# A graph kernel on one core: table product moved up one step and behind the masks, tail written out by hand

## The reference, cut to what matters

```python
h = relu(layernorm(x))
s = adj @ h[:, 0]
x = x + relu(h @ w_self.T + s[:, None] * w_neigh.sum(1))      # first layer
g = relu(layernorm(x))
Wh = (g @ W).reshape(n, 4, 64)                                # second layer
e = leaky_relu(sl[:, :, None] + sr.T[None]); masked by adj + eye
x = x + elu(softmax(e) @ Wh)
```

## Time and profile before

| | |
|---|---|
| median of 3 runs | 1017.08 us (1015.75 to 1019.13) |
| the profiled execution | 1017.7 us, its span 1015.9 us |
| mean granted clock of TensorE | 0.857 of full speed |
| busy: PE, DVE, ACT, POOL | 703.0, 709.7, 329.3, 398.5 us |
| last half of `adj` packed | 705.9 us into the span |
| last `write_rows` begins | 731.5 us |
| second half begins | 733.6 us |

### The profile page before, as it was taken

The page is one execution under the profiler, slowest core; times in us unless marked ns, Lnnn a source line. Parts: engine busy times, 40 slices in busy tenths (PEclk is TensorE's granted clock), DMA queues, the critical chain, the costliest instruction groups (busy, mean ns, idle before and its releaser), DMA issues.

```text
span 1015.9 us, 13279 instructions
## 1 busy us (share of the span) xinstructions
PE 703.0 (69%) x3025; PEld 465.6 (46%) x3026; DVE 709.7 (70%) x2868; ACT 329.3 (32%) x1353; POOL 398.5 (39%) x459
## 2 busy tenths in 40 slices
PE   1267777877678776787777878776536766777766
PEld 1134444544345443544444445443425655566555
DVE  6657676676766767667766676677537787778776
ACT  1023334343433434334343343333503232223221
POOL 0032323223232232322323223232277777777770
PEclk9979898889988899887888787889759799879788
DMA  9999999999999999999999999993134454444441
GB/s 301 416 421 416 424 421 426 420 423 420 425 423 422 422 421 422 407 400 419 398 424 407 416 404 408 412 416 146 55 95 130 122 149 133 132 133 132 139 120 56
DMA packets 69999, 321.93 MB, mean 317 GB/s; under 512 B 14498, under 2 KB 48721, under 8 KB 53536
## 3 DMA queue, kind: packets, MB, share of 16 engines
q1 hardware_dynamic: 44160, 293.88, 71.0%
q0 software_dynamic: 15360, 17.46, 7.0%
q10 hardware_dynamic: 10400, 9.74, 2.8%
HBM read 312.57 MB, written 17.07 MB: 324 GB/s over the span
## 4 chain that ended last, share of the span: by engine, by line
DMA 56%; PE 14%; issue 11%; POOL 11%; DVE 4%; SPq 2%; ACT 0%; POOLq 0%; ACTq 0%; DVEq 0%
DMA big<-in_adj_dram 54%; POOL big L904 11%; PE p_pack L674 10%; SPq L247 2%; PE p_u L945 2%; DMA x_rows<-in_x_dram 1%; DMA big<-row_table,lists 1%; PE p_u L946 1%; PE p_row L661 1%; DVE big L1051 0%; DVE big L1072 0%; POOLq L904 0%; PE p_row L945 0%; DVE stat L321 0%; PE p_u L639 0%
## 5 line engine op out<-in xcount | busy, mean ns | idle before, releaser
L674 PE MATMUL p_pack<-big,pack_w 128*128 128x512 fp8e5 x1024 | 307.9, 452 | 159.1 <-DMA big<-in_adj_dram 144.5
L294 POOL DMA_INDIRECT h0g<-h_table,nbr x192 | 191.7, 998 | 472.3 <-ACT nbr L528 387.1
L674 PEld LDWEIGHTS p_pack<-big,pack_w 128*128 128x128 fp8e5 x1024 | 103.4, 107 | 307.3 <-issue 228.2
L904 POOL DMA_INDIRECT big<-row_table,lists x192 | 197.9, 1031 | 75.2 <-issue 57.3
L362 DVE MAX8 tops<-p_pack 128x8 f32<-128x256 f32 x128 | 48.9, 423 | 153.1 <-PE p_pack L674 153.1
L492 ACT ACTIVATE nbr<-keys 128x2 uint32<-128x2 f32 x64 | 13.0, 203 | 373.7 <-DVE keys L397 373.7
L945 PE MATMUL p_u<-big,ident 128*128 128x256 f32 x288 | 92.6, 469 | 57.1 <-DVE big L1072 57.1
L945 PEld LDWEIGHTS p_u<-big,ident 128*128 128x128 f32 x288 | 66.3, 238 | 72.1 <-DVE big L1072 60.3
L639 PE MATMUL p_u<-wselfT,hT 128*128 128x256 f32 x256 | 78.9, 439 | 0.0
L661 PE MATMUL p_row<-w_gat_and_heads,gT 128*128 128x264 f32 x256 | 69.4, 395 | 0.6 <-ACT rows L572 0.6
L1051 DVE TENSOR_TENSOR big<-big,p_pack 128x768 f32<-128x768 f32 x64 | 58.2, 950 | 1.1
(11 more groups left out here) (145 smaller groups left out, 1338.7 us busy)
## 6 DMA issues: line engine op xcount, KB each, us to landing
big<-in_adj_dram SPq DMA_DIRECT2D x128, 2048.0 KB, 18.2
row_table<-rows ACTq DMA_DIRECT2D x64, 132.0 KB, 9.5
big<-row_table SPq DMA_DIRECT2D x32, 264.0 KB, 3.0
x_rows<-in_x_dram SPq DMA_DIRECT2D x8, 1024.0 KB, 12.4
out_dram<-big SPq DMA_DIRECT2D x32, 256.0 KB, 2.8
h0g<-h_table,nbr POOLq DMA_INDIRECT x192, 6.2
big<-row_table,lists POOLq DMA_INDIRECT x192, 2.8
big<-in_L_gnn_w_self_dram ACTq DMA_DIRECT2D x1, 256.0 KB, 5.1
```

The lines of the kernel that those rows point to most:

```text
L294: nc.gpsimd.indirect_dma_start(out=h0g[r][:, j:j + 1], out_offset=None, in_=h0_dram[:, :], in_offset=bass.IndirectOffsetOnAxis(ap=nbr[r][: ...
L674: last = nc.tensor.matmul(p_pack[:], pack_w[:, block_no, :], low_bytes(n % HALVES)[:, i, :], start=(block_no == 0), stop=(block_no == BLOC ...
L904: nc.gpsimd.indirect_dma_start(out=dst, out_offset=None, in_=row_dram[:, :], in_offset=bass.IndirectOffsetOnAxis(ap=lists[r][:, a, j:j + 1 ...
```

## The change

`table_product` goes from lag 6 at the head of the step to lag 5 between `first_places` and `pack_second`; `write_rows` goes from lag 6 to 5, behind `second_norm`. GpSimd asks for the extra neighbour of tile t-1 behind the direct ones of tile t. What comes behind the last packing is written out for each engine (`last`), with `map_extras` ahead of `update`. The `first_product` of tile 63 goes into the bank `p_pack` and waits for the last search in place of the `update` before. `sum_flags` is called once.

```diff
-            def run(eng, *stages):
+            def run(eng, *stages, last=()):
...
-                for t in range(total + max(lag for _, lag in stages)):
+                for t in range(total + (0 if last else max(lag for _, lag in stages))):
                     step(t // depth, t % depth)
+                for stage, t in last:
+                    stage(t // depth, t % depth)
...
+        def first_bank(k, r):
+            return p_pack if num(k, r) == TILES - 1 else p_first
...
-            run(pool, (gather, 0))
+            run(pool, (ask_direct, 0), (ask_extra, 1))
...
-            run(dve, (name_extras, 2), (update, 4), (map_extras, 1), (norm, 4), (search, 0), (sort, 0), (mark, 0))
+            z = TILES - 1
+            run(dve, (name_extras, 2), (update, 4), (map_extras, 1), (norm, 4), (search, 0), (sort, 0), (mark, 0),
+                last=((name_extras, z - 1), (map_extras, z), (update, z - 3), (norm, z - 3), (name_extras, z),
+                      (update, z - 2), (norm, z - 2), (update, z - 1), (norm, z - 1), (update, z), (norm, z)))
...
             run(act, (list_neighbours, 1), (count_extras, 1), (keep_maps, 2), (pick_extras, 2),
-                (first_norm, 2), (copy_hT, 3), (copy_gT, 5), (deviation, 4), (write_rows, 6), (second_norm, 4))
+                (first_norm, 2), (copy_hT, 3), (copy_gT, 5), (deviation, 4), (second_norm, 4), (write_rows, 5),
+                last=((copy_hT, z - 2), (copy_gT, z - 4), (first_norm, z - 1), (list_neighbours, z), (count_extras, z),
+                      (keep_maps, z - 1), (pick_extras, z - 1), (write_rows, z - 4), (deviation, z - 3), (copy_hT, z - 1),
+                      (second_norm, z - 3), (first_norm, z), (keep_maps, z), (pick_extras, z),
+                      (deviation, z - 2), (second_norm, z - 2), (copy_gT, z - 3), (copy_hT, z), (write_rows, z - 3),
+                      (deviation, z - 1), (second_norm, z - 1), (copy_gT, z - 2), (write_rows, z - 2),
+                      (deviation, z), (second_norm, z), (copy_gT, z - 1), (write_rows, z - 1), (copy_gT, z), (write_rows, z)))
...
-                if not (isinstance(t, int) and t == 0):
+                if t == TILES - 1:
+                    pe.wait_ge(searched, TILES)
+                elif t > 0:
...
-            run(pe, (spread_extras, 2), (turn_first, 3), (sum_flags, 3), (first_product, 4), (turn_second, 5), (table_product, 6),
-                (pack_first, 0), (first_places, 1), (pack_second, 0))
+            z = TILES - 1
+            run(pe, (spread_extras, 2), (turn_first, 3), (first_product, 4), (turn_second, 5),
+                (pack_first, 0), (first_places, 1), (table_product, 5), (pack_second, 0),
+                last=((spread_extras, z - 1), (turn_first, z - 2), (first_product, z - 3), (turn_second, z - 4),
+                      (first_places, z), (table_product, z - 4), (turn_first, z - 1), (spread_extras, z),
+                      (first_product, z - 2), (turn_second, z - 3), (table_product, z - 3), (turn_first, z),
+                      (first_product, z - 1), (turn_second, z - 2), (sum_flags, z), (first_product, z), (table_product, z - 2),
+                      (turn_second, z - 1), (table_product, z - 1), (turn_second, z), (table_product, z)))
```

More of the change, by code:

```diff
@@ L284, in gpsimd_fill_lists, with ask, ask_direct @@
             pool.wait_ge(h0_out, 16)
-            def gather(k, r):
+            def ask(r, j):
+                nc.gpsimd.indirect_dma_start(
+                    out=h0g[r][:, j:j + 1], out_offset=None, in_=h0_dram[:, :],
+                    in_offset=bass.IndirectOffsetOnAxis(ap=nbr[r][:, j:j + 1], axis=0),
+                    bounds_check=N - 1, oob_is_err=False).then_inc(h0_in[r], 16)
+            def ask_direct(k, r):
                 t = num(k, r)
@@ L291, in gather, with ask_extra @@
                 wait_alone(pool, h0g_clear, t + 1)
[L293 to L297, removed]
                 wait_alone(pool, direct_ready, t + 1)
                 for j in range(DIRECT):
-                    ask(j)
-                wait_alone(pool, extra_ready, t + 1)
-                ask(DIRECT)
-            run(pool, (gather, 0))
+                    ask(r, j)
+            def ask_extra(k, r):
+                wait_alone(pool, extra_ready, num(k, r) + 1)
+                ask(r, DIRECT)
+            run(pool, (ask_direct, 0), (ask_extra, 1))
         def vector_fill_lists(dve):
@@ L448, in update @@
                 dve.wait_ge(h0_in[r], (k + 1) * 16 * OWN)
-                step(nc.vector.scalar_tensor_tensor(stot[r][:], h0g[r][:, 0:1], h0g[r][:, 1:2], p_first[:, D:D + 1],
+                step(nc.vector.scalar_tensor_tensor(stot[r][:], h0g[r][:, 0:1], h0g[r][:, 1:2], first_bank(k, r)[:, D:D + 1],
                                                     ALU.add, ALU.add), 1)
-                step(nc.vector.scalar_tensor_tensor(y[r][:], vsum[:], stot[r][:], p_first[:, 0:D], ALU.mult, ALU.add), 2)
+                step(nc.vector.scalar_tensor_tensor(y[r][:], vsum[:], stot[r][:], first_bank(k, r)[:, 0:D], ALU.mult, ALU.add), 2)
                 step(nc.vector.scalar_tensor_tensor(x_tile(k, r), y[r][:], 0.0, x_tile(k, r), ALU.max, ALU.add), 3)
@@ L634, in first_product @@
                 pe.wait_ge(hT_ready, t + 1)
-                if not (isinstance(t, int) and t == 0):
+                if t == TILES - 1:
+                    pe.wait_ge(searched, TILES)
+                elif t > 0:
                     pe.wait_ge(upd_step, (t - 1) * UPD + 2)
                 for c in range(DC):
-                    nc.tensor.matmul(p_first[:, 0:D], hT[r][:, c * P:(c + 1) * P], wselfT[:, c, :],
+                    nc.tensor.matmul(first_bank(k, r)[:, 0:D], hT[r][:, c * P:(c + 1) * P], wselfT[:, c, :],
                                      start=(c == 0), stop=(c == DC - 1))
@@ L642, in first_product @@
                 pe.wait_ge(map_copied, t + 1)
-                nc.tensor.matmul(p_first[:, D:D + 1], map_[r][:], h0g[r][:, DIRECT:OWN], start=True, stop=True
+                nc.tensor.matmul(first_bank(k, r)[:, D:D + 1], map_[r][:], h0g[r][:, DIRECT:OWN], start=True, stop=True
                                  ).then_inc(u_ready, 1)
@@ L678, in sum_flags @@
             def sum_flags(k, r):
-                if num(k, r) != TILES - 1:
-                    return
                 pe.wait_ge(flagged, TILES)
```

## The result

The changed kernel takes **1071.44 us** (median of 3 runs, 1068.44 to 1085.22), the kernel before beside it 1017.08. The ratio is 1.0518, 95% interval 1.0481 to 1.0555: **slower by 5.2%, 54 us**. The forecast was 1036.6 with a range of 1016 to 1050: the sign was right, the size was not. The profiled execution is the longest, 14 us over the median, and counts as slow, while the ratio goes by the fast ones (1068.44 to 1071.44), so its parts add up to some 14 us more than the ratio says.

The account below looks back on a forecast made before the run. Landings of `adj` loads, 10.53 us a tile, were taken to bound the stream. 731.5 + 16 (ring) + 3.5 (tail) + 284.4 = 1035.4 us span; with 1.8 around it, less 0.6 to the median, 1036.6; range 1016 to 1050.

Parts of the forecast that it names:

- the ring: Stream: waits from second packing through `sort`, `list_neighbours`, `copy_gT` and table product to the next second packing; +16 us.
- The mean of the ring: Stream: average distance between second packings, forecast 10.8 us, 0.27 over the landings' pace, +16 us over 60 tiles.
- all low time falls on the pair: Stream: upper bound with all 2.7 us low-clock time on table product and second packing; 10.9 us a tile, +22.
- three tiles in five wholly low: Stream: bound with 0.6 of tiles at 12.2 us, mean 11.2, +40 us, 1060; grouped with a 0.05 rival.
- every pass starts slow: Stream: rival with product and packing low at every step, 12.2 us a tile, +100, 1120 us; chance 0.05.
- The loads: Stream: `adj` loads asked for later once TensorE is behind, but not lost: two tiles (21 us) against 17.8.
- The split gathers: GpSimd: extra neighbour asked for behind the direct ones lands some 2 us later, due two steps on; costs nothing.
- The tail, +3.5: After the last packing: high-clock walk of the written order gave +0.5, low stretches raised it to +3.5; bounds -4, +7.
- the +1.9: Tail: table product and `first_product` alone behind a wait, each nearly doubled by the low clock.
- The rest, 284.4: From the last copy of table rows to the end of the span: 284.4 us, untouched by the change.
- The ring keeps up: Stream: rival with the clock high on product and packing, so only the tail loses; 1020.6 us; chance 0.14.
- Faster by the tail alone: Tail: rival with one round of table rows less and the earlier map kept, -4, 1013 us; chance 0.11.

Follow-up runs that it names:

- `copies_first`: Changed kernel with ScalarE's `copy_hT` and `copy_gT` moved to the head of its step, ahead of the wait for the sort; 1024.66 us, ratio 1.0075.
- `ring_only`: Kernel before with only the stream's new order (table product at lag 5 before `pack_second`, rows at lag 5), old tail and gathers; 1071.61 us, ratio 1.0549.
- `one_filler`: Changed kernel with one extra 512-column matmul per step, ahead of `first_places`, into a bank nobody reads; 1044.18 us, ratio 1.0217.
- `tail_only`: Changed kernel with the stream's old order (table product and rows at lag 6), keeping the written-out tail and split gathers; 1024.24 us, ratio 1.0063.
- `filled_pauses`: Changed kernel with extra 512-column matmuls in each step, 3 ahead of `first_places` and 4 behind, order and waits kept; 1024.10 us, ratio 1.0070.
- `new_tail_old_gathers`: `copies_first` with TensorE's and ScalarE's written-out tail lists reordered, and neighbours asked for as in the kernel before; 1016.10 us, ratio 0.9990.
- `old_stream_new_tail`: Kernel before's stream and gathers with the written tails of `new_tail_old_gathers`, tile 58's product and rows added; 1016.58 us, ratio 0.9968.

## Why the prediction was right in sign and wrong in size

**The mechanism.** Right as far as the ring and what releases whom. Second packings are released by the table product and that by `copy_gT`; 59 waits show it, and `copies_first` gives the time back when that wait goes. The way from one packing's end to the copy's was 6.79 us for 6.78.

**The two lengths of the ring.** Right: 9.79 for a forecast 9.68 at the high clock, 12.38 for 12.2 at the low one.

**The mean of the ring, "10.8 us, near the upper bound" of 10.9.** This is the step that failed. It took the low time from the kernel before, 0.26 of the time or 2.7 us a tile, as fixed, and asked only where it would fall. In the changed kernel it is 0.38 of 11.55, **4.4 us a tile**. By the step's own formula (9.68 + 0.45 x 4.4) that alone gives 11.7, close to the 11.55 measured. It fits the two other profiles with a slow ring as well: `ring_only` has 0.31 of 11.29, 3.5 us a tile, which gives 11.3; `one_filler` 0.26 of 10.96, 2.85 us, which gives 10.96. So "all low time falls on the pair", the step's upper bound, was nearly the case, and what it lacked was the low time itself. These 4.4 us are of the longest execution. For the median one, 47 us over 60 tiles put the ring at 11.3 us and, by the same formula, the low time at some 3.6 us a tile; that is an estimate. With the old order it is 2.8 us a tile in the first profile of the kernel before, 2.2 in the second and 3.2 in `tail_only`, so part of the distance to 4.4 is spread. The low share answers to the pauses, and the change had altered those: in the earlier trace rows the table product stood between two blocks of work, now it stands alone behind 1.57 us of waiting, with `first_places` as the only work in 3 us. `filled_pauses` (0.03 low, nothing late) and `one_filler` (0.26, 27 us less) show it. The term came to +64.5 in the profile for a forecast +16; the largest of its bounds, "three tiles in five wholly low", was +40 and stood among the rivals with 0.05. The mix was in fact heavier: 22 of 58 steps at 12.38 and 28 more at 11.18 or 11.43. Three low packings in five, read in the earlier trace rows, had been the nearest rows and should have set the forecast, though +40 falls short too. Counted over all 61 second packings from tile 3 on, 44 already take over 2.0 us in the kernel before (35 in its second profile), and 54 do in the changed kernel: five packings were a small sample.

**The page's rule, "every pass starts slow", 1120 us.** The Trainium skill, "TensorE: Matmul & The Clock Gate", section "HAM oscillation", says that a matmul loop which waits some 3 to 5 us for data in each pass has its clock taken back each time and starts each pass slow. That is a near case and not "just this", as the prediction has it: no wait on this ring is longer than 1.6 us. The trace agrees in kind and not wholly in degree: 50 of 58 passes were longer than the high one, but 8 were at 9.79, and of the others only 22 were low on both product and packing.

**The loads.** Right: "once TensorE is behind" they are asked for later and still come in time; two waits for a landing are left, and the DMA share of 0.96 is the one named.

**The split gathers, the list order of ScalarE, the bank of tile 63.** Costed at nothing. For the gathers `new_tail_old_gathers` shows it; the other two were not tried alone.

**The tail, +3.5.** Near: +4.7 in the profile, +4.8 in that of `tail_only` (some 2 more against the second profile of the kernel before), whose other 3 us of 7 lie in a later last packing (708.7). The walk held well. With 64.5 for the later last packing taken off, `copy_gT` of 60 ends at 719.0 (forecast 719.1). These are its stages in the changed kernel:

```profile
783.21 0.35 ACT L575 COPY gT<-p_gT 128x256 f32<-128x256 f32 x1
```

```profile
783.61 2.13 PE L681 MATMUL p_row<-w_gat_and_heads,gT 128*128 128x264 f32 x4 [2.79 <-ACT gT L575]
...
785.96 1.92 PE L659 MATMUL p_u<-wselfT,hT 128*128 128x256 f32 x4
```

The product alone behind a wait and the `first_product` behind it are low (2.13 and 1.92), as the +1.9 had it. `update` of 62 begins at 788.03, 17.6 us behind the last packing where it was 15.3; a walk at the high clock had put it at 15.5.

**The rest, 284.4.** Right to 1.7 us.

**The rivals.** "The ring keeps up" holds only where the pauses are filled or the copy comes earlier (1024 to 1025, with the 7 us of `tail_only` over the kernel before). "Faster by the tail alone" named as its condition that the copy of 60 isn't held. With that mended the tail falls from 29.5 to 23.1 us, 0.7 to 2.5 under that of the kernel before, and the kernel with it (1020.39) is still not faster.

## What to carry to other kernels

When a product moves between two urgent blocks of an in-order queue, follow its operand back through the other engines; if the way leads to the same queue, it is a ring, and its length goes against the pace of the stream, at the high clock **and** at the low one, since what it lacks adds up in every pass. If the two lengths lie on either side of the pace, don't take the share of low time from the kernel before: look whether the change leaves TensorE with little work among its pauses, and count the passes that are low already. Where such a ring can't be avoided, an operand copied earlier in its engine's list, or cheap matmuls in the pause, are worth trying before anything larger.

## What the hardware showed that was not expected

- The ring, once slow, keeps itself going in a fixed pattern: steps of 12.38 and 11.43 us take turns for up to fourteen tiles, broken by 11.18 and 9.79. The low stretch comes at a different place of the product and the packing each time, yet always at one of these few.
- One matmul of 512 columns (its row reads 0.38 us; rows of three and of four take 0.81 and 1.02, so each adds 0.21) in a step of 11 us took 27 us off the kernel. The pause that it shortens goes from 1.05 to 0.82 us. What exactly the chip looks at can't be read from these runs.
- No pause of the ring is longer than 1.6 us, and the clock still fell to 0.81 on average. The kernel before has pauses for landings of 1.0 to 4.0 us and was granted 0.87; `copies_first`, with 96 such pauses of up to 3.0 us, 0.92.
- With the slow ring an execution's time follows its granted clock: `one_filler` took 1032.9 us at 0.881 (mean of the whole span) and 1048.1 at 0.858, `ring_only` 1063.2 at 0.846 and 1076.1 at 0.830, the changed kernel 1068.4 at 0.838 and 1085.2 at 0.821. Executions of these three lay 13 to 17 us apart, those of the kernel before 7 to 11, those of `copies_first` and `filled_pauses` 2.
- Open are the reason for the pattern's four lengths, and 1 to 3 us of the last packing: all versions with the new place of the product in which landings set the pace show them (708.4 to 710.2, for 705.9 to 707.3 in the kernel before), but `tail_only` with the old place does too (708.7), and `old_stream_new_tail` does not (706.9).
